# Softmax attention: a score ring of four one-bank slots in place of two two-bank slots

## The reference

```
xn = layer_norm(x, w, b)                       # per token, D = 256
q, k, v = xn @ Wq + bq, xn @ Wk + bk, xn @ Wv + bv   # 16 heads of 16 columns
scores = q @ k.T + mask                        # per batch and head: 512 x 512
probs  = softmax(scores, axis=-1)
y = probs @ v
h = silu(layer_norm(y) * (1 + scale) + shift)
x = x + h @ W_out + b_out
```

## Time and profile before

| | |
|---|---|
| Timed runs | 3866.88, 3852.82, 3865.28 us; median 3865.28 |
| Span of the profiled execution | 3873.2 us |
| PE busy | 2902.1 us (75%) |
| DVE busy | 2801.5 us (72%) |
| ACT busy | 2089.7 us (54%) |
| POOL busy | 1716.0 us (44%), none of it in the attention batches |
| Mean granted TensorE clock | 0.830 of full speed |
| DVE maxima from the ring (L1346) | 256 instructions, 312.7 us busy |
| ACT exponentials from the ring (L1499) | 256 activations, 261.7 us busy |
| Ring matmuls (L1614, L1623) | 512 and 512, 193.0 and 189.3 us busy |

### The profile page before, as it was taken

The page is one execution under the profiler, slowest core; times in us unless marked ns, Lnnn a source line. Parts: engine busy times, 40 slices in busy tenths (PEclk is TensorE's granted clock), DMA queues, the critical chain, the costliest instruction groups (busy, mean ns, idle before and its releaser), DMA issues. The chain is left out here.

```text
span 3873.2 us, 38272 instructions
## 1 busy us (share of the span) xinstructions
PE 2902.1 (75%) x11060; PEld 1488.6 (38%) x11060; DVE 2801.5 (72%) x3410; ACT 2089.7 (54%) x3166; POOL 1716.0 (44%) x1209
## 2 busy tenths in 40 slices
PE   6999667877777877468788878866776866867775
PEld 4555333444444444222333322223434434434443
DVE  1333279999999999755555555515999989999996
ACT  0223267777777777213444444426766756767663
POOL 0000047678677768800000000003767667677686
PEclk7899787988988988768888888768887978878888
DMA  2000111111011101043333333010101011111011
GB/s 78 11 33 22 47 39 44 39 44 50 28 44 50 50 23 55 33 82 63 60 39 66 66 61 61 12 58 33 43 24 60 30 53 50 39 45 61 23 55 49
DMA packets 101857, 176.64 MB, mean 46 GB/s; under 512 B 10219, under 2 KB 88827, under 8 KB 92563
## 3 DMA queue, kind: packets, MB, share of 16 engines
q1 hardware_dynamic: 97430, 161.65, 15.8%
q0 software_dynamic: 4224, 12.59, 1.0%
HBM read 139.69 MB, written 34.12 MB: 45 GB/s over the span
## 5 line engine op out<-in xcount | busy, mean ns | idle before, releaser
L965 POOL TENSOR_TENSOR l_h<-l_h,l_c_all 128x512 f32<-128x512 f32 x1024 | 1483.1, 1465 | 709.6 <-DVE l_h L896 688.5
L896 DVE TENSOR_TENSOR_SCAN l_h<-l_dA,l_ps_dbu 128x512 f32<-128x512 f32 x1024 | 1210.1, 1205 | 137.2 <-PE l_ps_dbu L1089 81.8
L1089 PE MATMUL l_ps_dbu<-ident,l_dub 128*128 128x128 f32 x4096 | 691.8, 303 | 282.8 <-DVE l_h L896 256.9
L767 ACT ACTIVATE l_dub<-l_duT,l_b_tok 128x512 f32<-128x512 f32 x1024 | 723.6, 711 | 281.5 <-PE l_ps_dbu L1089 281.5
L1089 PEld LDWEIGHTS l_ps_dbu<-ident,l_dub 128*128 128x128 f32 x4096 | 520.2, 154 | 783.0 <-DVE l_h L896 535.5
L781 ACT ACTIVATE l_dA<-l_dt,l_a_neg 128x512 f32<-128x512 f32 x1024 | 724.1, 711 | 0.2
L1076 PE MATMUL l_ps_y<-l_h,ident 128*128 128x512 f32 x1024 | 630.2, 702 | 104.5 <-DVE l_h L864 103.9
L1346 DVE TENSOR_REDUCE l_q_max<-l_ring 128x2 f32<-128x1024 f32 x256 | 312.7, 1224 | 335.7 <-PE l_ring L1614 332.9
L1499 ACT ACTIVATE l_probs<-l_ring 128x1024 f32<-128x1024 f32 x256 | 261.7, 1024 | 433.3 <-PE l_ring L1623 432.3
L864 DVE TENSOR_TENSOR l_h<-l_h 128x512 f32<-128x512 f32 x512 | 459.8, 901 | 26.1 <-POOL l_h L965 26.0
L925 POOL DMA_INDIRECT l_x_in<-x_dram,l_idx_x x32 | 33.2, 1038 | 951.8 <-DMA l_idx<-in_idx 938.7
(11 more groups left out here) (181 smaller groups left out, 3049.2 us busy)
## 6 DMA issues: line engine op xcount, KB each, us to landing
l_c_all<-c_rows_dram SPq DMA_DIRECT2D x64, 1024.0 KB, 4.8
l_res<-x_dram SPq DMA_DIRECT2D x24, 512.0 KB, 5.4
parts_dram<-l_parts SPq DMA_DIRECT2D x48, 256.0 KB, 2.8
l_qs<-parts_dram SPq DMA_DIRECT2D x48, 256.0 KB
l_ks<-parts_dram SPq DMA_DIRECT2D x48, 256.0 KB
l_x_in<-x_dram SPq DMA_DIRECT2D x16, 512.0 KB, 5.3
x_dram<-l_res SPq DMA_DIRECT2D x16, 512.0 KB, 3.0
su_cond_w<-in_cond_w SPq DMA_DIRECT2D x1, 5120.0 KB, 15.1
```

Of the source, the lines that this page charges most:

```text
L767: return act.activation(dub[:, n % 2, t, :], duT[:, p, t, :], ACT.Copy, scale=b_tok[:, p, t, n:n + 1])
L896: dve.tensor_tensor_scan(h[:, h_slot(s), :], dA[:, s % DA_RING, :], ps_dbu[:, dbu_slot(s), :], 0.0, ALU.mult, ALU.add).then_inc(scan_ok, 1)
L965: pool.tensor_tensor(h[:, h_slot(s), :], h[:, h_slot(s), :], c_all[:, (n // C_GROUP) % 2, n % C_GROUP, :], ALU.mult).then_inc(hc_ok, 1)
L1089: last = pe.transpose(ps_dbu[:, dbu_slot(s), t * P:(t + 1) * P], dub[:, n % 2, t, j * P:(j + 1) * P], ident[:])
```

## The change

`ring` becomes [P, 4, T]: RING = 4 slots of one bank. It holds the same four banks. A use is now one head: one matmul, one increment, one ACT or DVE instruction over 512 columns. For each step the order is E of head 0, M of head 0, E of head 1, M of head 1 (E0, M0, E1, M1), and each use waits for the reader of the use four before it, which is the same kind and head of the step before. All counts of `s_mm`, `smax_ok`, `exp_mm`, `exp_ok` become counts of heads (HEAD_USES = 64 for each batch). The first four uses of a batch wait each for one reader only. Nothing else moves between steps.

```
-RING = 2
+RING = 4
+HEAD_USES = 2 * PAIRS * TB
...
-        ring = ctx.enter_context(nc.psum_tensor("l2_ring", [P, RING, 2, T], F32))
+        ring = ctx.enter_context(nc.psum_tensor("l2_ring", [P, RING, T], F32))
...
-                    dve.tensor_reduce(q_max[:, pair // 2, i:i + 2, t], ring[:, slot, :, :], AX.X, ALU.max).then_inc(smax_ok, 1)
+                    dve.tensor_reduce(q_max[:, pair // 2, i, t:t + 1], ring[:, slot, :], AX.X, ALU.max).then_inc(smax_ok, 1)
...
-                        act.activation(probs[:, pair % GH, :, t, :], ring[:, n % RING, :, :], ACT.Exp).then_inc(exp_ok, 1)
-                        n += 2 if i < HALF_USES or has_next else 1
+                        for half in range(2):
+                            act.wait_ge(exp_mm, b * HEAD_USES + 2 * i + half + 1)
...
+                            act.activation(probs[:, pair % GH, half, t, :], ring[:, n % RING, :], ACT.Exp).then_inc(exp_ok, 1)
+                            n += 2 if i < HALF_USES or has_next else 1
...
-                        else:
-                            pe.wait_ge(exp_ok, b * U + RING)
-                            pe.wait_ge(smax_ok, b * U + HALF_USES + RING)
+                        elif first(b):
+                            pe.wait_ge(smax_ok, 2 * HALF_USES + RING)
+                        elif n % 2 == 0:
+                            pe.wait_ge(exp_ok, b * HEAD_USES - 1 + n // 2 + RING)
+                        else:
+                            pe.wait_ge(smax_ok, b * HEAD_USES + 2 * HALF_USES - 1 + n // 2 + RING)
...
-                    for i in range(U):
-                        slot_free(len(uses))
-                        exp_scores(b, p, i, len(uses) % RING)
-                        uses.append((exp_ok, b * U + i + 1 + RING))
...
+                    for i in range(2 * HALF_USES):
+                        for half in range(2):
+                            slot_free(len(uses))
+                            exp_scores(b, p, i, half, len(uses) % RING)
+                            uses.append((exp_ok, b * HEAD_USES + 2 * i + half + 1 + RING))
+                            if i < HALF_USES or has_next:
...
+                                slot_free(len(uses))
+                                max_scores(bb, p if i < HALF_USES else 1 - p, u, half, len(uses) % RING)
+                                uses.append((smax_ok, bb * HEAD_USES + 2 * u + half + 1 + RING))
```

More of the change, by code:

```diff
@@ L1338, in max_parts, with maximum @@
                     dve.tensor_tensor(m_parts[:, g, 2, :], m_rest[:], m_parts[:, g, 1, :], ALU.subtract).then_inc(m3_ok, 1)
-                def maximum(b, u, slot):
+                def maximum(b, u, half, slot):
                     pair, t = u // TB, u % TB
-                    dve.wait_ge(s_mm, b * PAIRS * TB + u + 1)
-                    if u % (2 * TB) == 0 and not first(b):
+                    dve.wait_ge(s_mm, b * HEAD_USES + 2 * u + half + 1)
+                    if u % (2 * TB) == 0 and half == 0 and not first(b):
                         dve.wait_ge(m_tr, (b - 1) * GROUPS + pair // 2 + 1)
-                    i = 2 * (pair % 2)
-                    dve.tensor_reduce(q_max[:, pair // 2, i:i + 2, t], ring[:, slot, :, :], AX.X, ALU.max).then_inc(smax_ok, 1)
+                    i = 2 * (pair % 2) + half
+                    dve.tensor_reduce(q_max[:, pair // 2, i, t:t + 1], ring[:, slot, :], AX.X, ALU.max).then_inc(smax_ok, 1)
                 def products_out(b, g):
@@ L1391, in run @@
                     for i in range(2 * HALF_USES):
-                        n += 1
-                        if i < HALF_USES:
-                            maximum(b, HALF_USES + i, n % RING)
+                        for half in range(2):
                             n += 1
-                        elif has_next:
-                            maximum(b + 1, i - HALF_USES, n % RING)
-                            n += 1
+                            if i < HALF_USES:
+                                maximum(b, HALF_USES + i, half, n % RING)
+                                n += 1
+                            elif has_next:
+                                maximum(b + 1, i - HALF_USES, half, n % RING)
+                                n += 1
                         if i in (14, 22, 30): products_out(b, i // GU - 1)
@@ L1440, in _ @@
                 for u in range(HALF_USES):
-                    maximum(0, u, u % RING)
+                    for half in range(2):
+                        maximum(0, u, half, (2 * u + half) % RING)
                     if u == 10:
@@ L1495, in run @@
                         pair, t = i // TB, i % TB
-                        act.wait_ge(exp_mm, b * PAIRS * TB + i + 1)
-                        if i % GU == 0 and not (first(b) and i < 2 * GU):
-                            act.wait_ge(pv_ok, b * GROUPS + i // GU - 1)
-                        act.activation(probs[:, pair % GH, :, t, :], ring[:, n % RING, :, :], ACT.Exp).then_inc(exp_ok, 1)
-                        n += 2 if i < HALF_USES or has_next else 1
+                        for half in range(2):
+                            act.wait_ge(exp_mm, b * HEAD_USES + 2 * i + half + 1)
+                            if i % GU == 0 and half == 0 and not (first(b) and i < 2 * GU):
+                                act.wait_ge(pv_ok, b * GROUPS + i // GU - 1)
+                            act.activation(probs[:, pair % GH, half, t, :], ring[:, n % RING, :], ACT.Exp).then_inc(exp_ok, 1)
+                            n += 2 if i < HALF_USES or has_next else 1
                         if has_next and i in (7, 8): v_part(b + 1, 1 - p, i - 7)
@@ L1590, in times_v @@
                     if m == 0:
-                        pe.wait_ge(exp_ok, b * PAIRS * TB + (g + 1) * GU + RING)
+                        pe.wait_ge(exp_ok, b * HEAD_USES + (g + 1) * 2 * GU + RING)
                         pe.wait_ge(v_ok, b * OUT + OUT)
@@ L1606, in turn, with max_scores, exp_scores @@
                     last.then_inc(y_tr, 1)
-                def max_scores(b, p, u, slot):
+                def max_scores(b, p, u, half, slot):
                     pair, t = u // TB, u % TB
-                    if u == 0:
+                    if u == 0 and half == 0:
                         pe.wait_ge(stack_ld, (b + 1) * 16 * 13)
[L1612 to L1617, removed]
+                    hd = 2 * pair + half
+                    pe.matmul(ring[:, slot, :], qs[0:MAX_AT, p, hd, t * P:(t + 1) * P], ks[0:MAX_AT, p, hd, :], start=True, stop=True).then_inc(s_mm, 1)
+                def exp_scores(b, p, u, half, slot):
                     pair, t = u // TB, u % TB
-                    if u % (2 * TB) == 0:
+                    if u % (2 * TB) == 0 and half == 0:
                         pe.wait_ge(m_ld[pair // 2], b * 48 + 48)
[L1621 to L1624, removed]
+                    hd = 2 * pair + half
+                    pe.matmul(ring[:, slot, :], ks[:, p, hd, t * P:(t + 1) * P], qs[:, p, hd, :], start=True, stop=True).then_inc(exp_mm, 1)
                 @batches
                 def run(b, p, has_post, has_next, has_after):
-                    U = PAIRS * TB
                     uses = []
@@ L1647, in run @@
                             reader[ps_o.name] = (res_ok, b * OUT - OUT)
-                    for i in range(U):
-                        slot_free(len(uses))
-                        exp_scores(b, p, i, len(uses) % RING)
-                        uses.append((exp_ok, b * U + i + 1 + RING))
-                        if i < HALF_USES or has_next:
-                            bb, u = (b, HALF_USES + i) if i < HALF_USES else (b + 1, i - HALF_USES)
-                            slot_free(len(uses))
-                            max_scores(bb, p if i < HALF_USES else 1 - p, u, len(uses) % RING)
-                            uses.append((smax_ok, bb * U + u + 1 + RING))
+                    for i in range(2 * HALF_USES):
+                        for half in range(2):
+                            slot_free(len(uses))
+                            exp_scores(b, p, i, half, len(uses) % RING)
+                            uses.append((exp_ok, b * HEAD_USES + 2 * i + half + 1 + RING))
+                            if i < HALF_USES or has_next:
+                                bb, u = (b, HALF_USES + i) if i < HALF_USES else (b + 1, i - HALF_USES)
+                                slot_free(len(uses))
+                                max_scores(bb, p if i < HALF_USES else 1 - p, u, half, len(uses) % RING)
+                                uses.append((smax_ok, bb * HEAD_USES + 2 * u + half + 1 + RING))
                         if has_post and 2 <= i < 2 + TB: times_v(b - 1, 1 - p, GROUPS - 1, i - 2)
@@ L1686, in _ @@
                 for u in range(HALF_USES):
-                    if u >= RING:
-                        pe.wait_ge(smax_ok, u + 1)
-                    max_scores(0, 0, u, u % RING)
+                    for half in range(2):
+                        if 2 * u + half >= RING:
```

(2 more changed lines are left out.)

4 lines of the change are left out of this document (2 added, 2 removed).

## The result

The changed kernel takes 3757.1 us (median of 4 runs, 3750.4 to 3779.2) against 3861.9 before: the ratio is 0.973, 95% interval 0.970 to 0.977. The sign was right, the size was not.

The account below looks back on a forecast made before the run. PE was taken to bound the steps with `times_v` (half of 32), the readers' round trip the others. Finer hand-over gave 35 us and the clock 6: 3865.3 - 41 = 3824 us, range 3782 to 3858.

Parts of the forecast that it names:

- Durations: Reader instructions on one head: a DVE maximum takes 0.687 us, an ACT exponential 0.59 (bounds 0.587 and 0.683).
- The prologue: Maxima ahead of the batches, bound by DVE: 16 uses 1.28 us apart instead of 1.177, 1.6 us lost.
- Finer hand-over: Each step at full clock: first half ready after 0.42 us; exponentials end 0.15 sooner, maxima 0.33 sooner.
- Turn's wait: Steps 6, 14, 22, 30, PE waiting for DVE's copy: 1.99 us shrinks to 1.66, 1.3 us a batch.
- Steps 9 to 12: First exponential half frees E0(10) sooner and the maxima of step 12 follow: 0.8 us a batch gained.
- The 0.4 for `result`: PE's wait for `result` (2.01 us) stands behind a maximum, so 0.4 us a batch gained.
- 9.6 us more in each batch (64 x 0.150): DVE's added work from halved maxima, said to lie in its 47 us of idle time a batch.
- The sum without the clock: Ordinary batch gains 5.05 us: head 2.25, turns 1.3, steps 9 to 12 0.8, `result` 0.4, other waits 0.3; 35 in all.
- The clock: Clock staying up at batch heads would give 7 x 3.4 = 24 us; a quarter of it, 6, was counted.
- No change: Rival: step gains are waited for at the next fixed point behind PE's stream and DVE's long jobs; 3848 us, chance 0.14.
- Slower: Rival: DVE becomes the bound in every step, 0.150 us for each of 256 double maxima, 38 us; 3903, chance 0.06.
- Clock recovered: Rival: denser head keeps TensorE at 2.4 GHz, all 24 us and as much again elsewhere; 3785 us, chance 0.10.

Follow-up runs that it names:

- E1: Not a run: in the changed kernel's step order E0, M0, E1, M1 it is E of head 1; no time of its own.
- before_fill: Kernel before plus four extra bf16 matmuls ahead of each turn's wait, into the bank the turn overwrites: 3815.2 us, ratio 0.985.
- before_fill_all: Kernel before plus filler matmuls at the turns and ahead of the waits of steps 13, 16, 20 and 21: 3796.9 us, ratio 0.979.
- order_eemm: Changed kernel with order E0 E1 M0 M1 in place of E0 M0 E1 M1, still four one-head slots: 3798.5 us, ratio to before 0.981.
- max_halves: Order E0 E1 M0 M1 in four slots; DVE reduces one head at a time, ACT takes both in one instruction: 3841.0 us, ratio to before 0.997.
- exp_halves: Order E0 E1 M0 M1 in four slots; ACT takes one head at a time, DVE both in one instruction: 3872.5 us, ratio to before 1.002.
- after_fill: Changed kernel plus the same four filler matmuls ahead of each turn's wait: 3721.9 us, ratio to before 0.963.
- before_head: Kernel before with only the joint wait of a batch's first two uses split, each waiting for one reader: 3867.5 us, ratio 1.001.
- after_early: Changed kernel with DVE's copy of ps_y ahead of the maxima of steps 6, 14, 22, 30: 3723.3 us, ratio to before 0.964.
- before_early: Kernel before with DVE's copy of ps_y ahead of the maxima of steps 6, 14, 22, 30: 3788.7 us, ratio 0.982.
- early_fill: Changed kernel with the earlier ps_y copy and the fillers of steps 13, 16, 20 and 21: 3711.4 us, ratio to before 0.960.
- pairs_head: Changed kernel's counting and one-reader head waits, order E0 E1 M0 M1, ACT and DVE each reading both banks in one instruction: 3890.0 us, ratio to before 1.006.

## Why the prediction was wrong

Its steps, in its order:

- **Durations.** 0.687 and 0.59 forecast, 0.682 and 0.596 measured. Right. The rule of the Trainium skill that the prediction set against the split (page "ScalarE: Activation LUTs", section "Rules for kernel authors") is given there for an activation with a bias operand. These exponentials have none, and two halves took 1.19 us, not the 1.45 worked out from it.
- **The prologue.** I gave it 1.28 us a use; 22 halves took 13.24 us, so 1.20 instead of 1.177 before. Over-priced: 0.3 to 0.4 us lost, not 1.6. Halves start 0.60 apart, 0.08 under their duration, not 0.05.

```profile
1698.01 13.24 DVE L1347 TENSOR_REDUCE l_q_max<-l_ring 128x1 f32<-128x512 f32 x22
```

- **Finer hand-over.** 0.42 to the reader's start: right. Turn's wait 1.66 forecast, 1.62 measured. `times_v` steps 1.97, unchanged (steps 5, 11, 28, 29). Steps 9 to 12 gained 0.94 in the mean of batches 1 to 6, forecast 0.8. Steps 20 and 21 gained 0.13 each. Right. The 0.4 for `result` can't be read: its step 16 was at 1.2 GHz, all or in part, in every batch before. One figure was wrong and fed nothing: DVE's "9.6 us more in each batch (64 x 0.150)" prices each of 64 heads at what a pair costs; 32 pairs make 4.8, and DVE's busy time in batch 2 rose by 1.8 (61.82 to 63.62), since neighbours overlap.
- **The sum without the clock.** 5.05 us a batch forecast, 5.2 measured as the difference of the bases. For the layer: 100.1 us less 0.37 x 174 = 64 leaves 36, forecast 37 for the batches. Right, to a degree that some luck must have a part in: the error of a base is some 0.5 us, and where its two main parts came from (DVE's side and the alternation, about half each) I had not seen.
- **The clock.** This is the step that failed: "I take a quarter, 6". Low time fell by 174 us, and that was worth 64. The prediction had even its bound too low ("7 x 3.4 = 24", and for the rival "as much again"). In its sum it looked for low time at the heads alone. Low time for each batch, mean of batches 1 to 6:

| us at 1.2 GHz in | steps 31, 0 to 3 | steps 14 to 18 | steps 24 to 27 | whole batch |
|---|---|---|---|---|
| before | 10.5 | 21.9 | 4.5 | 38.9 |
| after | 2.8 | 15.4 | 0.6 | 19.9 |
| before_fill | 7.5 | 8.6 | 2.3 | 18.9 |
| before_fill_all | 9.1 | 0.0 | 3.4 | 12.5 |
| order_eemm | 1.7 | 17.1 | 3.2 | 24.5 |
| max_halves | 8.5 | 21.3 | 3.3 | 34.1 |
| exp_halves | 7.4 | 20.8 | 4.6 | 33.0 |

The heads alone lost 7.7 us, at 0.37 worth 2.8, close to the 3.4 of which I took a quarter. Another 11 us went elsewhere, most of it at steps 14 to 18 (a turn, `project_out`, `xn_half`), which held over half of the low time and which I had not priced. Of these kernels the head loses most of its low time only where both readers are halved (after, order_eemm), not with one of them and not with fillers; the fillers clear steps 14 to 18. The prediction also set the denser PE against the waits that remain ("the turn waits remain at 1.66 us"), as if a wait of 1.66 did the same as one of 2.0. The fillers speak against that: idle times of 1.05 in place of 2.0 at the turns took 139 us of low time from the kernel before. What 1.66 in place of 1.99 does by itself no run shows, so which of the shortened idle times took how much of the 174 us stays open.
- **The rivals.** No change: the ring's own part alone would have been 1%, so it falls. Slower: DVE kept 224.3 us of idle time before its maxima (335.7 before); it falls. DVE's ring maxima took 15.2 us more in all, not 38. Clock recovered was the right one, with a chance of 0.10; it should have been the forecast. Its time, 3785, was still 28 too high.

Two rules bear on this. The Trainium skill, page "TensorE: Matmul & The Clock Gate", section "A second HAM failure mode: psum-queue depth-cycling", describes a bf16 kernel of 512-column matmuls that cycles through PSUM banks, in which small idle times of PE between the groups make the clock swing. I passed it over. This case's traces agree: low time of 315 us in the kernel before, with no idle time of PE over 2.1 us in these batches. In the same page of the Trainium skill, section "HAM oscillation — how this bites in real kernels", the sentence that double-buffering of PSUM "gave no further gain" is on a kernel that the prediction calls dense; the page gives it 43.2% of peak. It does not carry over: here four slots in the same four banks gave 2.7%.

What stays open: why the low time splits among batches as it does. after has 7, 14, 17, 27 and 27 us of it in batches 1 to 5, with the same instructions in each. And whether the change in low time between two kernels can be forecast from a trace at all; where I gave a number for it, it was right in four runs (before_fill, after_fill, exp_halves, before_head) and missed in five (before_fill_all, after_early, before_early, early_fill, max_halves), and in pairs_head it rose where I expected it to shrink.

## What to carry to other kernels

Where TensorE swings between its two levels, price the clock first: split the batches' lengths into a base and a slope over their low time (here 0.37), and reckon that an idle time of TensorE that an edit shortens can be worth more than its own length (it need not be: 0.62 us at each head gave nothing in before_head). A few matmuls into a bank that is about to be overwritten, placed ahead of a wait, test this in one run and cost nothing if they end before the wait does; here they gave 1.5% by themselves. When a ring serves two readers by turns, try the kinds in alternation, and one bank at a time for the reader that others wait for. In this kernel halving the other reader alone gave nothing, but the heads kept their clock only with both halved.

## What the runs showed of the hardware

- More matmuls, less time: 124 filler matmuls shortened the same batches by 48 us, with the granted clock up from 0.81 to 0.89.
- One us at 1.2 GHz costs a batch 0.37 us here, over 14 kernels whose bases differ by 10 us.
- An exponential of 512 columns out of PSUM without a bias takes 0.596 us, of 1024 columns 1.024. The form with a bias and 512 columns took 0.683.
- Consecutive DVE halves start 0.60 apart at a duration of 0.68, ACT's five in 2.90 us (head of batch 2) 0.58 apart at 0.60.
- A pair of matmuls with a wait and an increment on each reaches its reader 0.06 to 0.08 us later than with one of each for the pair (0.70 against 0.64 for ACT, 0.71 against 0.63 for DVE).
